# The first expert stage of a four-layer network: rows gathered by a slot table, results scattered tile by tile, no zeroed scratch

## The chip, the cores and the metric

The kernel runs on one core of a Trainium2 chip. The metric is the device time of one execution in microseconds, and below it is the median of several. The profile is one execution; its engines are PE (TensorE: matmuls, with PEld for its weight loads), DVE (VectorE), ACT (ScalarE), POOL (GpSimd) and SP (SyncE, which here only issues transfers). A row that ends in q (SPq, POOLq) is a queue from which transfers are issued.

## What is computed

A stream x of 16 x 64 tokens (1024 tokens, 256 values each) goes through four layers. Each layer adds a cross attention over 16 contexts of 1601 rows, a second attention or a scan, and a feed-forward part. The change concerns the feed-forward part of layer 0, and one side job in the cross attention of layer 0:

```python
def _L0_ffn_ref(hidden_states, gate_w, gate_bias, Wg, Wu, Wd, Sg, Su, Sd):
    E = 64
    TOP_K = 8
...
    x = hidden_states.reshape(B * S, H)
    rw = _route(x, gate_w, gate_bias)
    expert_out = jax.vmap(lambda gw_, uw_, dw_: _mlp(x, gw_, uw_, dw_))(Wg, Wu, Wd)
    routed = jnp.einsum('eth,te->th', expert_out, rw)
    shared = _mlp(x, Sg, Su, Sd)
    out = (routed + shared).reshape(B, S, H)
```

Each token picks 8 of 64 experts, each expert is a small gated network (256 to 176 to 256), and one shared network of 352 hidden values runs for all tokens.

## The kernel before

The stages run one after the other, with a barrier between two of them. `routed_experts` (from L1392) is the stage of the experts. Its inputs are `xn` (`nf_xn` in the profile), the 1024 normalised tokens as 8 tiles of 128 rows, the routing weights `score` and the choice `mask`. The 8192 pairs of a token and one of its experts are sorted by expert; each expert's pairs fill whole tiles of 128 slots, which needs at most `ROUTED_TILES` = 127 tiles, and all 127 are always computed. `owner_i` holds the expert of each tile, and `slot_i` (`e_sloti`) the slot of each pair.

In order:

- DVE computes slots and owners in a chain of short operations (`link` waits for each), fed by two matmuls that count the mask (L1561, L1562). These wait for the two constants on `const_in`.
- PE, ACT and DVE run a software pipeline over `UNITS` = 16 + 127 units: 16 shared units (two per token tile, weights `ws`), then one unit per routed tile. In loop step n, PE turns the rows of unit n+3 (`turn`, L1519), multiplies gate and up of unit n+2 (`gate_up`, L1532), turns the hidden values of n+1 (`turn_hidden`, L1541) and multiplies down of unit n (`down`, L1555). DVE copies turned rows (`take_rows`), multiplies gate by up (`multiply`), and takes results (`take_output`).
- The rows reach their slots through DRAM: POOL scatters `xn` to `routed_x` with 64 indirect transfers of 128 rows of 1 KB (L1500), then SP loads `routed_x` in 16 loads of 8 tiles (`load_rows`, L1465). Results go in 32 stores of 4 tiles to `routed_y` (L1491).
- SP's loop waits for `y_ready` of tile j, then loads the weights of tile j+7 (L1469, 608 KB), and at times rows or results.
- When everything is stored, POOL gathers back with 64 indirect transfers (L1507), and DVE adds each of them, scaled by the pair's weight, to `x` (L1671). A ring of 16 buffers lies between.
- `find_weights` (L1649 to L1652, three DVE operations for each of 8 token tiles) finds the weight of each pair. It stands before the first `take_rows`.

Slots that no pair fills would hold what was in memory, so `routed_x` is set to zero before: in the cross attention of layer 0, SP writes 16 blocks of 1 MB of zeros (`x_zero`, L468) among the loads of the contexts, and POOL waits for `net.cleared` before its first scatter.

## Time and profile before

| | |
|---|---|
| time, median of 3 | 4475.74 us (4473.22 to 4480.47) |
| the profiled execution | 4455.4 us, its span 4453.6 us |
| PE busy | 3800.3 us, 85% of the span |
| DVE, ACT, POOL busy | 2224.7, 1781.0, 684.8 us |
| the stage of the experts | 928.5 to 1447.7 us of the span |
| mean granted TensorE clock | 0.919 of full speed |

The span counts from the first to the last recorded instruction; the time of the execution is 1.8 us longer. A row of the order of time begins with start and duration in us, then engine, line, operation, output and inputs; in brackets is how long its engine was idle before and what ended that. "issue" is idle time in which the engine waited for nothing that the profile shows. A row of a table of stretches has for each engine the busy us and the number of instructions, then the granted clock of PE (1.00 is full speed), the mean busy share of the 16 DMA engines, and GB/s.

### The profile page before, as it was taken

Reading aid. Unit: us, or ns where it says so; the run is one execution under the profiler, and the core shown is the slowest. Engines: PE = TensorE matmul, PEld = TensorE weight load, DVE = VectorE, ACT = ScalarE, POOL = GpSimd, SP = SyncE. Lnnn points to the kernel's source line nnn. Section 1 sums busy time; section 2 is a strip of 40 time slices with the busy share of each in tenths; the row PEclk is TensorE's granted clock in tenths of the full one; section 3 lists DMA queues with packets and bytes.
Section 4 is the critical chain, followed back from the end, with each engine's and each line's share of the span. In section 5 each row is a group of like instructions: output and inputs, shape, how many; then the busy total and the mean of one; then the engine's idle time right before and its main releaser. Section 6 shows DMA issues by size and latency. Waiting matters only on the chain. (4 is left out here: it accounts for less than half of the span.)

```text
span 4453.6 us, 141607 instructions
## 1 busy us (share of the span) xinstructions
PE 3800.3 (85%) x64078; PEld 2972.4 (67%) x64078; DVE 2224.7 (50%) x4259; ACT 1781.0 (40%) x3676; POOL 684.8 (15%) x393
## 2 busy tenths in 40 slices
PE   7999998647992799999966889999963789999988
PEld 5777776525771588888725568777843678878865
DVE  4555554542443555555564355555544255555543
ACT  4555453211220345454413345555531244544431
POOL 1111110031005111111140011111112111111100
PEclk9999999668996899999987899999976899999998
DMA  3121210026994211111040111111013611010001
GB/s 102 51 84 58 68 60 12 8 102 241 352 351 133 62 47 35 47 37 45 3 114 2 32 60 47 40 40 47 18 27 140 207 53 48 33 48 33 34 11 33
DMA packets 109045, 330.29 MB, mean 74 GB/s; under 512 B 31680, under 2 KB 55760, under 8 KB 101632
## 3 DMA queue, kind: packets, MB, share of 16 engines
q1 hardware_dynamic: 98800, 299.61, 20.0%
q0 software_dynamic: 6912, 18.88, 1.3%
q8 instruction: 507, 8.31, 0.8%
q10 hardware_dynamic: 2736, 2.75, 0.2%
q14 instruction: 90, 0.74, 0.1%
HBM read 261.80 MB, written 51.00 MB: 70 GB/s over the span
## 5 line engine op out<-in xcount | busy, mean ns | idle before, releaser
L636 DVE TENSOR_REDUCE x_pm<-banks 128x4 f32<-128x1536 f32 (+2 forms) x512 | 935.6, 1827 | 1034.7 <-PE banks L547 1034.7
L759 ACT ACTIVATE x_kT<-banks,x_bk 128x384 f32<-128x384 f32 (+2 forms) x512 | 305.1, 596 | 915.1 <-PE banks L589 915.1
L744 ACT ACTIVATE x_pe<-banks 128x512 f32<-128x512 f32 (+1 forms) x1024 | 474.2, 549 | 194.2 <-PE banks L527 194.2
L576 PE MATMUL banks<-x_wh,x_ch 128*128 128x256 f32 (+1 forms) x1664 | 523.6, 315 | 9.7 <-issue 5.8
L482 POOL TENSOR_TENSOR x_cl<-xnT,x_ch 128x1601 fp32r<-128x1601 f32 x60 | 218.6, 3643 | 1769.5 <-ACT x_ch L749 1769.5
L744 ACT ACTIVATE x_pl<-banks 128x384 f32<-128x384 f32 x1024 | 419.8, 496 | 166.9 <-PE banks L527 166.9
L576 PE MATMUL banks<-x_wh,x_cl 128*128 128x256 f32 (+1 forms) x1664 | 470.3, 283 | 1.7 <-issue 1.6
L527 PE MATMUL banks<-x_q,x_kT 32*128 32x128 f32 x13312 | 470.9, 274 | 0.5 <-issue 0.5
L576 PE MATMUL banks<-x_wl,x_ch 128*128 128x256 f32 (+1 forms) x1664 | 468.5, 282 | 1.7 <-issue 1.5
L576 PEld LDWEIGHTS banks<-x_wh,x_ch 128*128 128x128 f32 (+1 forms) x1664 | 307.9, 185 | 206.1 <-ACT x_pl L744 94.4
L547 PE MATMUL banks<-x_kT,x_q 32*128 32x384 f32 (+2 forms) x4096 | 434.7, 497 | 11.3 <-ACT x_kT L759 4.5
L527 PEld LDWEIGHTS banks<-x_q,x_kT 32*128 32x128 f32 x13312 | 427.0, 182 | 3.1 <-issue 0.8
L589 PE MATMUL banks<-x_ch,x_wh 128*128 128x384 f32 (+2 forms) x1024 | 370.9, 362 | 45.0 <-DVE x_cl L730 43.9
L669 DVE TENSOR_TENSOR x_v<-banks,x_bv 128x256 f32<-128x256 f32 (+1 forms) x832 | 320.4, 417 | 171.5 <-PE banks L576 171.2
L589 PE MATMUL banks<-x_ch,x_wl 128*128 128x384 f32 (+2 forms) x1024 | 358.8, 350 | 0.0
L589 PE MATMUL banks<-x_cl,x_wh 128*128 128x384 f32 (+2 forms) x1024 | 358.2, 350 | 0.0
L576 PEld LDWEIGHTS banks<-x_wl,x_ch 128*128 128x128 f32 (+1 forms) x1664 | 309.3, 186 | 2.8 <-issue 2.8
L576 PEld LDWEIGHTS banks<-x_wh,x_cl 128*128 128x128 f32 (+1 forms) x1664 | 309.2, 186 | 1.7 <-issue 1.7
L561 PEld LDWEIGHTS banks<-x_pl,x_v 128*32 128x32 f32 (+1 forms) x12288 | 182.4, 110 | 114.4 <-ACT x_pe L744 78.0
L561 PEld LDWEIGHTS banks<-x_pe,x_v 128*32 128x32 f32 x14336 | 206.8, 110 | 75.9 <-ACT x_pl L744 69.4
L561 PE MATMUL banks<-x_pe,x_v 128*32 128x64 f32 x14336 | 228.8, 220 | 15.0 <-issue 5.0
L561 PE MATMUL banks<-x_pl,x_v 128*32 128x64 f32 (+1 forms) x12288 | 206.1, 221 | 40.4 <-issue 24.9
(371 smaller groups left out, 5538.6 us busy)
## 6 DMA issues: line engine op xcount, KB each, us to landing
e_w<-in_L_pack SPq DMA_DIRECT2D x127, 608.0 KB, 6.6
xnT<-in_ctxT SPq DMA_DIRECT2D x64, 800.5 KB, 4.4
x_raw<-in_ctxT SPq DMA_DIRECT2D x60, 800.5 KB, 5.8
e_w<-in_L_pack SPq DMA_DIRECT2D x21, 1154.0 KB, 7.5
routed_x<-x_zero SPq DMA_DIRECT2D x16, 1024.0 KB, 8.3
e_xt<-routed_x SPq DMA_DIRECT2D x16, 1024.0 KB, 8.0
routed_y<-e_y SPq DMA_DIRECT2D x32, 512.0 KB, 7.5
a_swap<-a_raw SPq DMA_DIRECT2D x64, 128.0 KB, 2.3
```

Of the source, the lines that this page charges most:

```text
L482: nc.gpsimd.tensor_tensor(cl[:, b % 2, k, 0:CTX], staged(b, k), ch[:, b % 2, k, 0:CTX], ALU.subtract).then_inc(low_done, 1)
L527: last = nc.tensor.matmul(mine[j][0:n, (t - lo) * P:(t - lo + 1) * P], kT[r, c, t * P:t * P + n], qb[r, u, c], start=False, stop=True, ski ...
L547: last = nc.tensor.matmul(into[j][:, 0:hi - lo], qb[r, u, c], kT[r, c, lo:hi], start=not masked, stop=True, skip_group_check=masked)
L561: last = nc.tensor.matmul(bank[32 * j:32 * j + 32, e * S:(e + 1) * S], v[0:w, u, t, at:at + 32], probabilities(j, t, t + 1)[0:w, 0, e * S: ...
L576: last = nc.tensor.matmul(bank[0:w, (t - lo) * D:(t - lo + 1) * D], x[:, u, c, t * P:t * P + w], y[:, 1, c, :], start=(c == m == 0), stop= ...
L589: last = nc.tensor.matmul(bank[:, 0:hi - lo], w[:, 0, i, c * P:(c + 1) * P], x[:, u, i, lo:hi], start=(i == n == 0), stop=(i == KC - 1 and ...
L636: nc.vector.tensor_reduce(pm[:, c, :, g], net.quads[1 - k % 2][:, :, 0:hi - lo], AX.X, ALU.max).then_inc(max_done, 1)
L669: ins = nc.vector.tensor_tensor(heads, bank[0:w, (t - lo) * D:(t - lo + 1) * D].rearrange("p (h e f) -> p h e f", e=2, f=16), bvb[0:w].rea ...
L744: nc.scalar.activation(probabilities(j, lo, hi).rearrange("p t q -> p (t q)"), sets[k % 2][j][:, 0:(hi - lo) * P], ACT.Exp).then_inc(exp_d ...
L759: nc.scalar.activation(kT[:, c, lo:hi], sets[k % 2][key_bank(k)][:, 0:hi - lo], ACT.Identity, bias=col[:, c:c + 1]).then_inc(k_taken, 1)
```

## The change

- The zeros, their 16 writes and their semaphore are gone, and so is the scatter of `xn` by POOL. `xn` is written to `routed_x` as it is, 1 MB in one transfer by SP.
- A table is built that tells for each slot which pair fills it. For each token tile DVE makes 8 matrices `of_tile` (the pair's number where the column is the pair's tile) and 8 matrices `of_row` (1 where the column is the pair's row in its tile), 128 x 128 each, and PE adds the 64 products up in one PSUM tile (`index(t)`, in the first 8 shared units). DVE turns it into `to_pair` and `to_token`; an empty slot gets a spare row of its own behind the pairs. A third constant (`pair_rows`, 160 KB) is needed, and the first counting matmuls wait for it too.
- POOL gathers the rows of each tile by `to_token` into a ring of 8 and scatters the results of each tile by `to_pair` out of a ring of 8: 127 and 127 indirect transfers of 128 rows of 1 KB, in turn, inside the loop.
- Results lie in the order of token and pair afterwards, so that SP loads them back with 8 plain transfers of 1 MB into a ring of 4, and DVE's 64 additions alternate between two token tiles, each waiting for the addition two before it.
- SP's weight loads wait for `down_done` and no longer for `y_ready`. `find_weights` runs inside the loop, after the output of every eighth unit from the first routed one.

PE, place: the first shared units. `e_ws`, `xnT` are the shared weights and the turned tokens, `e_h` and `e_hT` the hidden values. Before:

```order
L1561 MATMUL banks<-r_mask,e_before 128x512
L1562 MATMUL banks<-r_mask,ones 128x512
L1564 MATMUL banks<-ident,e_owner 1x128
L1532 MATMUL banks<-e_ws,xnT 128x352 x4
L1541 MATMUL banks<-ident,e_h 88x128 x2
L1532 MATMUL banks<-e_ws,xnT 128x352 x2
L1541 MATMUL banks<-ident,e_h 88x128 x2
L1555 MATMUL banks<-e_ws,e_hT 128x256 x2
```

PE, the same place in the changed kernel:

```order
L1520 MATMUL banks<-e_ws,xnT 128x352 x4
L1551 MATMUL banks<-e_oftile,e_ofrow 128x128 x8
L1529 MATMUL banks<-ident,e_h 88x128 x2
L1520 MATMUL banks<-e_ws,xnT 128x352 x2
L1551 MATMUL banks<-e_oftile,e_ofrow 128x128 x8
L1529 MATMUL banks<-ident,e_h 88x128 x2
L1543 MATMUL banks<-e_ws,e_hT 128x256 x2
```

Eight matmuls of the table stand between gate-and-up and the turning of the hidden values, in each of 8 units. DVE, the same place in the changed kernel (`e_place` is the pair's tile and row, `e_h` the product of gate and up):

```order
L1613 CAST e_place<-e_sloti 128x128
L1615 TENSOR_SCALAR e_owneri<-banks 1x128
L1623 TENSOR_SCALAR e_oftile<-e_pair,e_place 128x128 x8
L1626 TENSOR_TENSOR e_ofrow<-e_pair,e_place 128x1024
L1647 TENSOR_TENSOR e_h<-e_g,banks 128x176
L1623 TENSOR_SCALAR e_oftile<-e_pair,e_place 128x128 x8
L1626 TENSOR_TENSOR e_ofrow<-e_pair,e_place 128x1024
L1647 TENSOR_TENSOR e_h<-e_g,banks 128x176
```

The two products of `multiply` have the making of the ones ahead of them now. POOL, the stage, before:

```order
L1495 UNCONDITIONAL_BRANCH
L1500 DMA routed_x<-nf_xn,e_sloti 16384x256 x64
L1507 DMA e_yt<-routed_y,e_sloti 128x256 x64
L40 UNCONDITIONAL_BRANCH
L43 ISA x2
```

POOL, the start of the stage in the changed kernel:

```order
L1490 MEMSET e_xt 128x2048
L1482 DMA e_xt<-routed_x,e_totoken 128x256 x9
L1487 DMA routed_y<-e_y,e_topair 24576x256
L1482 DMA e_xt<-routed_x,e_totoken 128x256
L1487 DMA routed_y<-e_y,e_topair 24576x256
```

Two blocks outside the loop became one gather and one scatter per tile inside it. The diff, cut to its core:

```diff
-                if clear is not None:
-                    for n in range(b * CLEARS // (B - 2), (b + 1) * CLEARS // (B - 2)):
-                        rows = clear[n * CLEAR_TILES * P:(n + 1) * CLEAR_TILES * P, :].rearrange("(p j) n -> p (j n)", p=P)
-                        sp.dma_start(rows, zero[:]).then_inc(net.cleared, 16)
...
-    LOAD, X_RING = 8, 3
-    STORE, Y_RING = 4, 2
-    RING = 16
+    X_RING, Y_RING, BACK = 8, 8, 4
+    PAIRED = TILES * K
...
             def load_weights(j):
                 e = sp.value_load(owner_i[0:1, j:j + 1], min_val=0, max_val=E - 1)
                 sp.dma_start(w[:, j % SLOTS], d["L0_pack"][bass.ds(e, 1)].rearrange("o p n -> p (o n)")).then_inc(w_in[j % SLOTS], 16)
 
             sp.dma_start(before[:], d["before"]).then_inc(const_in, 16)
             sp.dma_start(const[:], d["sort_rows"]).then_inc(const_in, 16)
+            sp.dma_start(pair[:], d["pair_rows"]).then_inc(const_in, 16)
             sp.dma_start(ws[:], d["L0_shared"].rearrange("s p n -> p s n")).then_inc(shared_in, 16)
+            sp.dma_start(x_rows.rearrange("(t p) n -> p t n", p=P), xn[:]).then_inc(rows_out, 16)
             sp.wait_ge(tiles_known, 1)
             for j in range(SLOTS):
                 load_weights(j)
-            sp.wait_ge(scattered, 16 * TILES * K)
-            for n in range(X_RING):
-                load_rows(n)
-            for j in range(ROUTED_TILES):
-                sp.wait_ge(y_ready, j + 1)
-                if j + SLOTS < ROUTED_TILES:
-                    load_weights(j + SLOTS)
-                if j % LOAD == 0 and j and j // LOAD + X_RING - 1 < LOADS:
-                    load_rows(j // LOAD + X_RING - 1)
-                n = j // STORE
-                tiles = tiles_of(n, STORE)
-                if j == tiles.stop - 1:
-                    at = tiles.start % LOAD
-                    rows = grouped(y_rows)[j // LOAD][:, at:at + STORE]
-                    sp.dma_start(rows, y[:, n % Y_RING]).then_inc(stored[n % Y_RING], 16)
+            for j in range(SLOTS, ROUTED_TILES):
+                sp.wait_ge(down_done, SHARED + j - SLOTS + 1)
+                load_weights(j)
             for s in range(Y_RING):
-                sp.wait_ge(stored[s], 16 * ((STORES - s + 1) // Y_RING))
+                sp.wait_ge(stored[s], 16 * uses(Y_RING, s))
+            for t in range(TILES):
+                if t >= BACK:
+                    sp.wait_ge(added, K * (t - BACK + 2 - t % 2))
+                rows = y_rows[t * P * K:(t + 1) * P * K, :].rearrange("(p k) n -> p (k n)", p=P)
+                sp.dma_start(yt[:, t % BACK].rearrange("p k n -> p (k n)"), rows).then_inc(back[t % BACK], 16)
 
         @block.gpsimd
         def _(pool):
-            pool.wait_ge(net.cleared, 16 * CLEARS)
-            pool.wait_ge(slots_known, 1)
-            for n in range(TILES * K):
-                pool.indirect_dma_start(x_rows, bass.IndirectOffsetOnAxis(ap=slot_i[:, n:n + 1], axis=0), xn[:, n // K, :],
-                                        None).then_inc(scattered, 16)
-            for s in range(Y_RING):
-                pool.wait_ge(stored[s], 16 * ((STORES - s + 1) // Y_RING))
-            for n in range(TILES * K):
-                if n >= RING:
-                    pool.wait_ge(added, n - RING + 1)
-                pool.indirect_dma_start(yt[:, n % RING, :], None, y_rows,
-                                        bass.IndirectOffsetOnAxis(ap=slot_i[:, n:n + 1], axis=0)).then_inc(back[n % RING], 16)
+            def gather(j):
+                s = j % X_RING
+                if j >= X_RING:
+                    pool.wait_ge(turned, j - X_RING + 1)
+                pool.indirect_dma_start(xt[:, s], None, x_rows, bass.IndirectOffsetOnAxis(ap=to_token[:, j:j + 1], axis=0)).then_inc(x_in[s], 16)
+
+            def scatter(j):
+                s = j % Y_RING
+                pool.wait_ge(y_ready, j + 1)
+                pool.indirect_dma_start(y_rows, bass.IndirectOffsetOnAxis(ap=to_pair[:, j:j + 1], axis=0), y[:, s],
+                                        None).then_inc(stored[s], 16)
+
+            nc.gpsimd.memset(xt[:], 0.0).then_inc(rows_out, 1)
+            pool.wait_ge(rows_out, 17)
+            pool.wait_ge(index_known, 1)
+            for j in range(X_RING):
+                gather(j)
+            for j in range(ROUTED_TILES):
+                if j + X_RING < ROUTED_TILES:
+                    gather(j + X_RING)
+                scatter(j)
...
+            def index(t):
+
+                pe.wait_ge(ones_made, 2 * t + 2)
+                for k in range(K):
+                    last = nc.tensor.matmul(table, of_row[:, t % 2, k], of_tile[:, t % 2, k], start=(t == k == 0),
+                                            stop=(t == TILES - 1 and k == K - 1))
+                last.then_inc(ones_used, 1)
...
-            pe.wait_ge(const_in, 32)
+            pe.wait_ge(const_in, 48)
...
-                if n + 3 == SHARED:
-                    pe.wait_ge(slots_known, 1)
-                    pe.wait_ge(tiles_known, 1)
                 if SHARED <= n + 3 < UNITS:
                     turn(n + 3)
                 if 0 <= n + 2 < UNITS:
                     gate_up(n + 2)
+                if 0 <= n + 1 < TILES:
+                    index(n + 1)
...
-            link(nc.vector.tensor_scalar(spot_i[:, 0], slot[:].rearrange("p t k -> p (t k)"), -1.0, None, ALU.add))
-            link(nc.vector.tensor_scalar(spot_i[:, 1], spot_i[:, 0], P - 1, 3, ALU.bitwise_and, ALU.logical_shift_left))
-            link(nc.vector.tensor_scalar(spot_i[:, 2], spot_i[:, 0], 7, LOAD - 1, ALU.logical_shift_right, ALU.bitwise_and))
-            link(nc.vector.tensor_scalar(spot_i[:, 3], spot_i[:, 0], LOADS * LOAD * P - LOAD * P, None, ALU.bitwise_and))
-            link(nc.vector.tensor_tensor(spot_i[:, 1], spot_i[:, 1], spot_i[:, 2], ALU.bitwise_or))
-            nc.vector.tensor_tensor(slot_i[:], spot_i[:, 1], spot_i[:, 3], ALU.bitwise_or).then_inc(slots_known, 1)
+            link(nc.vector.tensor_scalar(slot_i[:, 0], slot[:].rearrange("p t k -> p (t k)"), -1.0, None, ALU.add))
+            nc.vector.tensor_scalar(slot_i[:, 1], slot_i[:, 0], 7, None, ALU.logical_shift_right).then_inc(chain, 1)
+            link_two = nc.vector.tensor_scalar(slot_i[:, 2], slot_i[:, 0], P - 1, None, ALU.bitwise_and)
+            done[0] += 1
+            link(link_two)
+            link(nc.vector.tensor_copy(place[:], slot_i[:, 1:3]))
             dve.wait_ge(owner_turned, 1)
             nc.vector.tensor_scalar(owner_i[:], count[0:1, 0:P], -1.0, None, ALU.add).then_inc(tiles_known, 1)
+
+            def ones(t):
+
+                if t >= 2:
+                    dve.wait_ge(ones_used, t - 1)
+                for k in range(K):
+                    n = t * K + k
+                    ins = nc.vector.tensor_scalar(of_tile[:, t % 2, k], pair[:, PAIRED:PAIRED + P], place[:, 0, n:n + 1], pair[:, n:n + 1],
+                                                  ALU.is_equal, ALU.mult)
+                ins.then_inc(ones_made, 1)
+                nc.vector.tensor_tensor(of_row[:, t % 2], spread(pair[:, PAIRED:PAIRED + P].unsqueeze(1), (P, K, P)),
+                                        spread(place[:, 1, t * K:(t + 1) * K].unsqueeze(2), (P, K, P)), ALU.is_equal).then_inc(ones_made, 1)
+
+            def index():
+
+                dve.wait_ge(ones_used, TILES)
+                link(nc.vector.scalar_tensor_tensor(spare[:], table, 0.0, pair[:, PAIRED + P:], ALU.is_equal, ALU.mult))
+                link(nc.vector.scalar_tensor_tensor(to_pair[:], table, -1.0, spare[:], ALU.add, ALU.add))
+                nc.vector.tensor_scalar(to_token[:], to_pair[:], 3, TOK - 1, ALU.logical_shift_right, ALU.bitwise_and).then_inc(index_known, 1)
...
-                s = j // STORE
-                if s >= Y_RING:
-                    dve.wait_ge(stored[s % Y_RING], 16 * (s // Y_RING))
-                nc.vector.tensor_copy(y[:, s % Y_RING, j % STORE], y_ps[o % 2][:, 0:D]).then_inc(y_ready, 1)
+                if j >= Y_RING:
+                    dve.wait_ge(stored[j % Y_RING], 16 * (j // Y_RING))
+                nc.vector.tensor_copy(y[:, j % Y_RING], y_ps[o % 2][:, 0:D]).then_inc(y_ready, 1)
 
             def find_weights(t):
                 u = t % 2
...
 
             for n in range(-3, UNITS):
                 if SHARED <= n + 3 < UNITS:
-                    if n + 3 == SHARED:
-                        for t in range(TILES):
-                            find_weights(t)
                     take_rows(n + 3)
+                if 0 <= n + 2 < TILES:
+                    ones(n + 2)
+                if n + 2 == TILES:
+                    index()
                 if 0 <= n + 2 < UNITS:
                     multiply(n + 2)
                 if n >= 0 and (n >= SHARED or n % 2):
                     take_output(n)
+                if n >= SHARED and n % 8 == 0 and (n - SHARED) // 8 < TILES:
+                    find_weights((n - SHARED) // 8)
             dve.wait_ge(weighted, TILES)
             dve.wait_ge(shared_added, TILES)
             for n in range(TILES * K):
-                t, k = n // K, n % K
-                dve.wait_ge(back[n % RING], 16 * (n // RING + 1))
-                if k:
-                    dve.wait_ge(added, n)
-                nc.vector.scalar_tensor_tensor(net.x[:, t, :], yt[:, n % RING, :], weight[:, t, k:k + 1], net.x[:, t, :], ALU.mult,
+                t, k = 2 * (n // (2 * K)) + n % 2, n // 2 % K
+                if k == 0:
+                    dve.wait_ge(back[t % BACK], 16 * (t // BACK + 1))
+                else:
+                    dve.wait_ge(added, n - 1)
+                nc.vector.scalar_tensor_tensor(net.x[:, t, :], yt[:, t % BACK, k], weight[:, t, k:k + 1], net.x[:, t, :], ALU.mult,
                                                ALU.add).then_inc(added, 1)
```

## Rows read from the trace of the kernel before

**Rows 1.** Table of stretches, in the stage of the experts.

```profile
941.00:976.00 35.00, 33.91 (x142) 23.84 (x140) 12.21 (x41) 8.80 (x29) 22.66 (x24) 0.96 0.57 208
976.00:992.00 16.00, 0.00 (x0) 0.00 (x0) 15.31 (x24) 0.00 (x0) 12.62 (x12) 0.55 0.28 97
992.00:1030.00 38.00, 0.00 (x0) 0.00 (x0) 0.00 (x0) 0.00 (x0) 27.89 (x29) 0.50 0.30 104
1100.00:1150.00 50.00, 49.81 (x241) 36.73 (x240) 21.88 (x60) 11.97 (x40) 0.00 (x0) 1.00 0.98 351
1368.00:1447.00 79.00, 0.00 (x0) 0.00 (x0) 30.52 (x63) 0.00 (x0) 58.63 (x62) 0.50 0.36 105
```

**Rows 2.** Order of time: PE at the start and end of the routed units.

```profile
974.82 1.03 PE L1555 MATMUL banks<-e_ws,e_hT 88*128 88x256 f32 x4
...
1035.06 0.66 PE L1519 MATMUL banks<-ident,e_xt 128*128 128x128 f32 x2 [59.21 <-DMA e_xt<-routed_x]
...
1039.61 0.38 PE L1519 MATMUL banks<-ident,e_xt 128*128 128x128 f32 x2
...
1354.38 0.38 PE L1519 MATMUL banks<-ident,e_xt 128*128 128x128 f32 x2
```

**Rows 3.** Order of time: the end of the stage, last result to last addition.

```profile
1361.29 0.42 DVE L1645 COPY e_y<-banks 128x256 f32<-128x256 f32 x1 [0.44 <-PE banks L1555]
1365.20 0.98 POOL L1507 DMA_INDIRECT e_yt<-routed_y,e_sloti  x1 [336.49 <-DMA routed_y<-e_y]
...
1368.12 0.48 DVE L1671 SCALAR_TENSOR_TENSOR x_tok<-e_yt,e_weight,x_tok 128x256 f32<-128x256 f32 x1 [6.40 <-DMA e_yt<-routed_y,e_sloti]
...
1447.20 0.48 DVE L1671 SCALAR_TENSOR_TENSOR x_tok<-e_yt,e_weight,x_tok 128x256 f32<-128x256 f32 x1 [0.87 <-DMA e_yt<-routed_y,e_sloti]
```

**Rows 4.** POOL's indirect transfers: durations in ns, first and last start; two single ones.

```profile
L1500 POOL DMA_INDIRECT routed_x<-nf_xn,e_sloti x64: 959/963/1218, 946.3 to 1027.7; - x64
L1507 POOL DMA_INDIRECT e_yt<-routed_y,e_sloti x64: 949/949/985, 1365.2 to 1444.3; - x64
...
975.71 1.22 POOL L1500 DMA_INDIRECT routed_x<-nf_xn,e_sloti  x1 [0.30 <-issue]
```

**Rows 5.** Layer 0's cross attention: a write of zeros, a gap of PE, clock.

```profile
316.48 0.91 SPq L468 DMA_DIRECT2D routed_x<-x_zero  x2
325.79 0.43 PE L561 MATMUL banks<-x_pl,x_v 65*32 65x64 f32 x5 [2.83 <-issue]
322.90:325.80 2.90, 0.07 (x5) 0.01 (x3) 0.28 (x1) 0.00 (x0) 0.00 (x0) 1.00 0.96 398
325.80:329.50 3.70, 3.70 (x16) 3.14 (x17) 1.63 (x6) 0.00 (x0) 0.00 (x0) 0.54 0.05 18
```

**Rows 6.** The batches' results (L694) in the cross attention of layers 0 and 2.

```profile
L694 DVE TENSOR_TENSOR actT<-x_num,x_rec x16: 291/292/293, 119.2 to 740.1; 128x128 f32<-128x128 f32 x16
L694 DVE TENSOR_TENSOR actT<-x_num,x_rec x16: 291/292/293, 2659.5 to 3261.6; 128x128 f32<-128x128 f32 x16
```

**Rows 7.** Order of time: single operations whose kind or size the change uses.

```profile
908.85 4.44 DVE L1366 MAX8 r_top<-r_choice 128x8 f32<-128x8 f32 x64
921.27 1.11 DVE L1377 MAX8 r_best<-r_choice 128x8 f32<-128x64 f32 x8
...
928.88 0.43 SPq L1472 DMA_DIRECT2D e_const<-in_sort_rows  x1
930.64 2.07 PE L1561 MATMUL banks<-r_mask,e_before 128*128 128x512 f32 x2 [23.26 <-DMA e_const<-in_sort_rows]
...
945.93 0.42 PE L1541 MATMUL banks<-ident,e_h 128*88 128x128 f32 x2 [0.94 <-DVE e_h L1633]
...
1030.18 1.28 SPq L1465 DMA_DIRECT2D e_xt<-routed_x  x3
...
3445.80 1.95 PE L1800 MATMUL banks<-e_xT,e_w 128*128 128x128 f32 x16
```

**Rows 8.** Their landing, from issue in us, scatter; then the issues by kind.

```profile
DMA to landing us min/median/max: 2.4/2.6/11.0
e_yt<-routed_y,e_sloti POOLq DMA_INDIRECT x64, 2.8
e_w<-in_L_pack SPq DMA_DIRECT2D x127, 608.0 KB, 6.6
```

**Rows 9.** DMA queues: software queue in 992 to 1029 and 1368 to 1447.

```profile
q0 software_dynamic: 1392, 3.80, 29.6%
...
q0 software_dynamic: 3024, 8.26, 36.3%
```

More of the change, by code:

```diff
@@ L473, in _ @@
                 nc.gpsimd.memset(side[:].bitcast(F32), 1.0).then_inc(side_set, 1)
-            if clear is not None:
-                nc.gpsimd.memset(zero[:], 0.0).then_inc(zero_set, 1)
             for u in range(2):
@@ L1445, in routed_experts @@
         cum, count = net.bank(0), net.bank(1)
-        def tiles_of(n, size):
-            return range(n * size, min(n * size + size, ROUTED_TILES))
-        def grouped(rows):
-            return rows.rearrange("(g p j) n -> g p j n", p=P, j=LOAD)
+        table = net.bank(0)[:, 0:P]
         def weights(n):
@@ L2602, in arrange @@
                                a["L0_ffn_Sd"].reshape(D, 2, 176).transpose(1, 0, 2))
+    pairs = 8 * np.arange(TOK).reshape(TILES, P, 1) + np.arange(1, 9)
+    o["pair_rows"] = np.concatenate([pairs.transpose(1, 0, 2).reshape(P, -1), np.tile(np.arange(P), (P, 1)),
+                                      8 * TOK + 1 + p[:, None] + P * np.arange(P)], 1).astype(f)
     o["sort_rows"] = np.concatenate([np.tile(P * np.arange(8), (P, 1)), p[:, None]], 1).astype(f)
```

62 lines of the change are left out of this document (29 added, 33 removed).

## The prediction

> **What bounds the kernel now.** I read the table of stretches first. In the stage of the experts PE works through the shared units (941 to 976), stands still from 976 to 1030 at a granted clock of 0.50 to 0.55, is busy 49.8 of 50 us in the routed loop, and stands still again from 1368 to 1447 [rows 1]. The order of time gives the edges. The last shared product ends at 974.82 + 1.03 = 975.85; the first turning of routed rows starts at 1035.06, after 59.2 us on the rows' load [rows 2]. The last turning starts at 1354.38, the second at 1039.61, so a unit takes 314.8 / 125 = 2.52 us. The last result is copied at 1361.29 + 0.42 = 1361.7, and the last addition ends at 1447.2 + 0.5 = 1447.7: a tail of 86.0 us without PE [rows 3]. In both pauses POOL sets the pace: the scatter starts its 64 transfers between 946.3 and 1027.7, and the reads back theirs between 1365.2 and 1444.3, so 79.1 / 63 = 1.255 us each; a scatter issue lasts 0.963 and has the same 0.30 idle before it, 1.267 [rows 4]. So 145 us of this stage are POOL's pace with PE idle, and only the loop is PE's.
>
> The other part is the cross attention of layer 0, which writes zeros. PE stops there for 2.83 us on nothing that the profile shows, in a stretch in which the DMA engines move 398 GB/s, 6.5 us after two blocks of zeros were issued; in the next 3.7 us its clock is 0.54 [rows 5]. From first to last batch result this stage takes 740.1 - 119.2 = 620.9 us, and the same code without zeros in layer 2 takes 3261.6 - 2659.5 = 602.1 [rows 6]. I read the difference, 18.8 us, as the zeros' price.
>
> **The front of the stage.** The wait of 59.2 us goes: no scatter of 64 steps stands before the loop. Its place is taken by the table.
>
> A third constant delays the first counting matmul. Before, that matmul started 930.64 - 928.88 = 1.76 us after the issue of the second constant [rows 7]; one more issue is 0.48 us and 160 KB take about 0.4 at 398 GB/s, so I take 1.0 (bounds 0.5 and 2.5).
>
> DVE makes the ones. 64 operations on 8 values take 4.44 us, 0.069 each, and 8 on 64 values 1.11, with the last one's tail 0.13 each [rows 7]; so about 0.06 + 1.04 ns per value, and `ones` is 8 x 0.19 + 1.13 = 2.7 us (3.7 if its eight do not overlap). PE's share has a direct row: eight 128 x 128 products in two passes each take 1.95 us at full clock [rows 7]. DVE needs 2.7 + 0.34 + 0.42 = 3.5 us per unit, PE 2.30 + 1.95 = 4.25 (2.30 is (975.85 - 945.93) / 13), so PE sets the pace of the eight units, and DVE shows only once, before the first: `ones(0)` starts at about 946.3 and ends at 949.1, `index(0)` ends at 951.05, and the first turning of hidden values, at 945.93 before [rows 7], stands at 951.05. That is 5.1; the seven other index steps add 7 x 1.95 = 13.7. The first routed turning comes at 975.85 + 18.8 = 994.6 and not 1035.06: **40.4 us gained**. The bounds are 33 (DVE the pace, the first index at half clock, the constant late) and 44.
>
> Are the rows there by then? `index(7)` ends at 951.05 + 7 x 4.25 = 980.8, three short DVE operations make 981.8, and a gather lands 2.8 us after issue [rows 8]: 984.6, ten before PE asks. The eighth is issued at 990.6 and wanted at 994.6 + 7 x 2.52. The write of `xn` (1 MB, issued about 930) is long over.
>
> PE comes to the loop warm. Before, the first routed turning and the second lay 4.55 us apart [rows 2], against 2.52: **2.0 gained**.
>
> **The loop.** Per unit POOL now issues a gather and a scatter, 1.255 + 1.267 = 2.52 us, exactly PE's 2.52. A ring covers differences. POOL issues the gather of tile j+9 after the scatter of j, which is about 1.7 units after loop step j begins, and PE turns that tile at step j+6: 4.3 units or 10.7 us later, of which 2.8 to 4 go to landing. So 7 us of lag are covered. Against PE's undisturbed 2.49 POOL would fall behind by 0.03 x 119 = 3.8, and `find_weights` slows it: in 976 to 992, with DVE on such operations, an issue is up to 1.22 and not 0.96 [rows 4], two per call, 8 calls, at most 4. I put the remaining stall at **1 us lost**. `find_weights` itself was hidden in the 59 us; 24 operations of 0.64 us (15.31 / 24) [rows 1], 1.9 per call, now delay the copy of turned rows. DVE works 21.9 of 50 us in the loop [rows 1], and the copy has one unit of lead less its own 0.4, so some 0.3 of each 1.9 reaches PE: **2.4 lost** (bounds 0 and 15).
>
> The DMA engines: they are busy 0.97 to 0.98 of the loop at 351 GB/s. Of a unit's 864 KB, 256 change from bulk to rows of 1 KB. The software queue took 29.6% of 37 us for 29 scatters, 0.38 each, and 36.3% of 79 for 62 reads, 0.46 each [rows 9]; the same 256 KB in bulk are 0.98 x 2.49 x 256 / 864 = 0.72. The sum rises by 0.12 us per unit if the share is a true load, to 2.56, which would be 5 to 10 us lost. But 398 GB/s were moved in [rows 5], so the 0.98 is partly queueing; I take 0, and 10 as the bound.
>
> **The tail.** The last result is scattered (issued at once, landed in 2.6 to 2.8), and SP issues the first 1 MB at +2.9. Before, the first of three such loads was wanted 1035.06 - 1030.18 = 4.9 after its issue [rows 2, 7]; each further MB takes 2.6 at 398 GB/s. DVE's addition of 256 values is 0.33 us apart if two tiles alternate (0.06 + 0.27), 0.49 at its full duration. Tiles 0 and 1 are there at +7.8 and +10.4, their 16 additions end at +15.3, tiles 2 and 3 at +20.7. Tiles 4 and 5 are issued at +15.4, there at 20.3 and 22.9, added by +27.7; 6 and 7 are there by 28.3 and added by +33. I take 34, with 42 at 0.49 each. Against 86.0: **52 gained** (43 to 54).
>
> **The zeros.** If the gaps are theirs, 18.8 is gained; the context loads remain, so I take **17** (bounds 0 and 20). Nothing hangs on the change of SP's weight wait: it comes earlier by one DVE copy.
>
> **Sum.** 40.4 + 2.0 - 1 - 2.4 + 52 + 17 = 108 us. The profiled execution becomes 4455.4 - 108 = 4347; it was 20.3 under the median of the runs, so against the median the forecast is 4475.7 - 108 = 4368 us.
>
> Two rules of the Trainium skill speak about POOL's transfers. The page "DMA: Bandwidth & Descriptors", section "Anatomy of one DMA — SWDGE (gpsimd) path", fits 2.0 us plus bytes / 436e3 to one such transfer, 2.3 for 128 KB; in series two would make 4.6 per unit and about 260 us lost by estimate. The trace agrees with the figure as landing time (2.6 to 2.8) and not as pace (1.255), so the sum keeps the pace.
>
> **Rivals.**
> - *DVE holds POOL off in the loop; slower.* In 976 to 992 POOL's issue grew from 0.96 to 1.22 while DVE worked on SBUF [rows 4]. If each of the three DVE operations of a unit (0.42, 0.41, 0.34) held back a full descriptor writing, POOL would need 2.52 + 1.17 = 3.7 per unit: (3.7 - 2.52) x 127 - 7 = 143 lost, 4511 us. It decides from 2.52 + (108 + 7) / 127 = 3.4 per unit. Against it: 24 issues ran beside such operations from PSUM in the shared units, 22.66 us busy or 0.94 each [rows 1]. The skill's page "SBUF — State Buffer", section "SBUF: two separate sides", has this rule: GpSimd can't write descriptors while DVE runs a two-port operation, fp32 copy within SBUF above all. The loop's copies read PSUM, and the row of 1.22 agrees with it only for operations within SBUF. Chance 0.03.
> - *POOL is the bound by a little.* Two kinds of transfer in turn, each with a wait, cost 2.6 to 2.8: (0.08 to 0.28) x 127 - 7 = 3 to 29 lost, 4371 to 4397, more if late rows let PE's clock fall. For it: the sum is level with PE without any margin. Chance 0.17.
> - *The zeros cost nothing;* the gaps come from the code's place and the context loads, and reappear: 17 less, 4385. Against it: layer 2's 602.1. Chance 0.12.
> - *DMA-bound loop,* 10 lost, 4378. Chance 0.08.
> - *The table is late or the rows of gaps in later stages shift:* other parts unchanged in code take 10 more. Chance 0.03.
>
> **How the numbers follow.** The forecast has 0.57, with 4350 to 4385 as its own range. Low end: 44 + 2 + 54 + 20 gained is 120, and later stages' gaps may give a few: 4350. High end: front 33, loop 15 lost, tail 43, zeros 10 is 73, 4403. The range 4350 to 4405 leaves out 0.2. Only the first rival ends slower: faster by over 0.2% (9 us, about what runs of this kernel can tell) 0.96, within it 0.01, slower 0.03.
>
> **What would show it.** The wait of the first routed turning under 5 us and its start near 995; eight units of 4.25 before it; the second turning 2.5 after the first; turnings 2.5 apart and POOL's issues 1.26 apart, with no wait for `e_xt` above 1 us in the loop; 34 us from the last `e_y` to the last `x_tok` of the stage; layer 0's batches over 602 to 605 us with no gap above 2 us. Wrong it would be if POOL's pairs take over 2.6 us, if PE waits for `e_xt` or `e_w` in most units, or if the 2.8 us gaps remain.

## The result, and the profile after

The changed kernel takes **4408.05 us** (median of 4 runs, 4403.77 to 4413.44) against 4477.57 for the kernel before on the same chip: ratio 0.9844, 95% interval 0.9828 to 0.9860. That is 69.5 us faster, where I forecast 108 (4368, range 4350 to 4405). The profiled execution took 4404.97 us, span 4403.1; that of before took 4455.4. Between the two profiled executions the difference is 50.4, and it is this one that the stretches below must add up to.

The front of the stage, in order of time (columns as in [rows 2]):

```profile
908.92 0.43 SPq L1458 DMA_DIRECT2D e_const<-in_sort_rows  x1
911.70 1.22 PE L1557 MATMUL banks<-r_mask,e_before 128*128 128x512 f32 x1 [24.28 <-DMA e_pair<-in_pair_rows]
926.14 2.12 DVE L1623 TENSOR_SCALAR e_oftile<-e_pair,e_place 128x128 f32<-128x128 f32 x8
928.18 1.21 DVE L1626 TENSOR_TENSOR e_ofrow<-e_pair,e_place 128x1024 f32<-128x1024 f32 x1
950.61 1.95 PE L1551 MATMUL banks<-e_oftile,e_ofrow 128*128 128x128 f32 x16
962.44 1.12 POOL L1482 DMA_INDIRECT e_xt<-routed_x,e_totoken  x1 [52.09 <-DVE e_totoken L1634]
975.32 0.39 PE L1508 MATMUL banks<-ident,e_xt 128*128 128x128 f32 x2
977.81 0.39 PE L1508 MATMUL banks<-ident,e_xt 128*128 128x128 f32 x2
```

The issue of the second constant stands at 908.92, against 928.88 [rows 7]: the stage starts 20.0 us earlier, and that is layer 0, whose batches' results (line 694 before, 684 now) last 720.4 - 119.2 = 601.2 us against 620.9 [rows 6]. From that issue to the first routed turning it is 66.4 us now and was 106.2 [rows 2, 7]: 39.8 gained, with no wait on the rows. The second turning comes 2.49 later.

```profile
L684 DVE TENSOR_TENSOR actT<-x_num,x_rec x16: 291/292/293, 119.2 to 720.4; 128x128 f32<-128x128 f32 x16
```

The tail (DVE waits four times for a load there, 11.7 us in all; two of the four are shown):

```profile
1366.31 0.42 DVE L1658 COPY e_y<-banks 128x256 f32<-128x256 f32 x1 [0.44 <-PE banks L1543]
1367.59 0.96 POOL L1487 DMA_INDIRECT routed_y<-e_y,e_topair  x1 [0.30 <-issue]
1370.14 2.14 SPq L1474 DMA_DIRECT2D e_yt<-routed_y  x4
1375.07 0.48 DVE L1688 SCALAR_TENSOR_TENSOR x_tok<-e_yt,e_weight,x_tok 128x256 f32<-128x256 f32 x1 [8.34 <-DMA e_yt<-routed_y]
1398.05 6.03 DVE L1688 SCALAR_TENSOR_TENSOR x_tok<-e_yt,e_weight,x_tok 128x256 f32<-128x256 f32 x15 [0.83 <-DMA e_yt<-routed_y]
```

From the end of the last copy, 1366.73, to 1398.05 + 6.03 = 1404.1 it is 37.4 us, against 86.0 [rows 3]: 48.6 gained. But between the first turning at 975.3 and the last at 1359.4 lie 384.1 us, against 1354.4 - 1035.1 = 319.3 [rows 2]: **64.8 lost**. Sum: 19.7 + 39.8 - 64.8 + 48.6 = 43.3, and the stages behind it give the other 7. Table of stretches (PE, PEld, DVE, ACT and POOL busy, PEclk, DMA share, GB/s), in the loop:

```profile
1100.00:1150.00 50.00, 43.87 (x199) 31.44 (x199) 21.33 (x56) 10.39 (x34) 31.68 (x32) 0.97 0.83 284
1200.00:1250.00 50.00, 44.04 (x191) 29.79 (x189) 17.33 (x47) 9.29 (x30) 32.08 (x33) 0.97 0.84 289
```

PE is busy 44 of 50 us and not 49.8, and nothing else has become full [rows 1]: the DMA engines fell from 0.98 to 0.83, POOL is at 32 of 50. The second row lies behind `find_weights`, and stalls just as the first does. No bound shows in this table, so one stall must be read in order of time:

```profile
1187.10 0.34 DVE L1647 TENSOR_TENSOR e_h<-e_g,banks 128x176 f32<-128x176 f32 x1 [1.00 <-issue]
...
1187.86 1.35 PE L1520 MATMUL banks<-e_w,e_xT 128*128 128x352 f32 x4
...
1189.05 0.97 POOL L1482 DMA_INDIRECT e_xt<-routed_x,e_totoken  x1 [0.31 <-issue]
1189.26 1.03 PE L1543 MATMUL banks<-e_w,e_hT 88*128 88x256 f32 x4
...
1190.32 0.98 POOL L1487 DMA_INDIRECT routed_y<-e_y,e_topair  x1 [0.30 <-issue]
1190.36 1.42 PE L1520 MATMUL banks<-e_w,e_xT 128*128 128x352 f32 x4
1191.61 0.97 POOL L1482 DMA_INDIRECT e_xt<-routed_x,e_totoken  x1 [0.30 <-issue]
1192.68 0.32 ACT L1698 ACTIVATE e_g<-banks 128x176 f32<-128x176 f32 x1 [5.33 <-PE banks L1520]
...
1193.43 0.42 PE L1529 MATMUL banks<-ident,e_h 128*88 128x128 f32 x2 [1.64 <-issue]
...
1194.16 0.43 DVE L1658 COPY e_y<-banks 128x256 f32<-128x256 f32 x1 [0.80 <-remote]
...
1194.87 0.98 POOL L1487 DMA_INDIRECT routed_y<-e_y,e_topair  x1 [2.29 <-DVE e_y L1658]
```

The gate and up product that starts at 1187.86 ends at 1189.21, but ACT, whose other wait (for `e_h`) was over at 1187.44, takes it at 1192.68. The down product ends at 1190.29, and DVE copies it at 1194.16. Then POOL, which had issued without a pause, gets its result, 2.29 us late. So what is late is TensorE's *signal*. I counted it from the trace's semaphore events, between 1050 and 1290 us: how long after the end of a product its increment is recorded. Before: 380 of 380 increments, mean 0.01 us, longest 0.02. After: 265 recorded for 309 products, 148 of them later than 0.1, mean 0.99, longest 4.73. Each increment is held against the latest product before it, so these delays are lower bounds. The increments of DVE and ACT that are recorded stand 0.01 us after their instructions, but over a third of those (DVE 93 of 249, ACT 54 of 156) are missing from the trace, so of them it is not shown.

POOL's issues have a pattern too: often six or eight, 1.28 us apart, then about 3 us to the next.

### The profile page after: what moved, and what is told of

Read it like the earlier page. It is cut to its first block and busy times, and to the rows that moved or that the text cites. A ratio compares the mean times of both kernels' runs of the same rounds, so it can differ in the third digit from the quotient of the medians.

```text
span 4403.1 us, 141949 instructions
## 1 busy us (share of the span) xinstructions
PE 3827.4 (87%) x64206; PEld 2983.3 (68%) x64206; DVE 2240.8 (51%) x4332; ACT 1781.4 (40%) x3676; POOL 809.2 (18%) x519
## 5 line engine op out<-in xcount | busy, mean ns | idle before, releaser
L472 POOL TENSOR_TENSOR x_cl<-x_raw,x_ch 128x1601 fp32r<-128x1601 f32 x60 | 181.0, 3017 | 368.5 <-ACT x_ch L739 368.5
```

Source lines behind the costliest of these rows:

```text
L472: nc.gpsimd.tensor_tensor(cl[:, b % 2, k, 0:CTX], staged(b, k), ch[:, b % 2, k, 0:CTX], ALU.subtract).then_inc(low_done, 1)
```

## The experiments

Each expectation is quoted as it stood before its run; the letters of the theories are explained where they first come. In the end theory D, which limits the number of indirect transfers in this loop to about one per 1.5 us, is what the runs left standing; it names no mechanism. Times are medians of 4 runs; "loop" is the time from the first to the last routed unit's down product, 126 units (314.0 us before, 380.8 in the changed kernel); "late" counts TensorE's increments between 1050 and 1290 us that were late as above, of those recorded.

**Plain loads.** SP loads 128 rows at a fixed place for every tile:

```diff
-                pool.indirect_dma_start(xt[:, s], None, x_rows, bass.IndirectOffsetOnAxis(ap=to_token[:, j:j + 1], axis=0)).then_inc(x_in[s], 16)
+                sp.dma_start(xt[:, s], x_rows[t * P:(t + 1) * P, :]).then_inc(x_in[s], 16)
```

> The changed kernel with its 128 row gathers made plain loads of 128 rows on SP's queue (the same 128 KB each, wrong rows, so the output is not the reference's); the 128 scatters stay on POOL. Measured in the changed kernel: 3.05 us per routed unit against 2.49 to 2.52 before, and 92 to 103 recorded signals of each kind of TensorE's (semaphore increments) that arrive with a median delay of 0.24 to 0.87 us and up to 4.7 us after the end of the matmul, against 0.02 us in the kernel before. Theory A (two indirect issues per unit, 1.28 us apart, hold TensorE's signals back, which then pass one every 0.74 us or so, four per unit): with one indirect issue per unit POOL pauses 1.2 us in each unit and the signals catch up: 2.5 to 2.6 us per unit, whole time 4345 to 4360. Theory B (the DMA engines have too much to do with weights, rows and results together): the bytes are the same, 4395 to 4410. Theory C (POOL's own pace of 2.56 us per unit, and its catching up): half the issues, 4340 to 4350, with no late signals at all.

4344.5 us, ratio to before 0.9710 (0.9694 to 0.9727). Loop 314.2, late 0 of 369.

**Plain stores.**

```diff
-                pool.indirect_dma_start(y_rows, bass.IndirectOffsetOnAxis(ap=to_pair[:, j:j + 1], axis=0), y[:, s],
-                                        None).then_inc(stored[s], 16)
+                sp.dma_start(y_rows[j * P:(j + 1) * P, :], y[:, s]).then_inc(stored[s], 16)
```

> The changed kernel with its 128 scatters made plain stores of 128 rows in slot order on SP's queue (results then stand at wrong rows, so the output is not the reference's); the 128 gathers stay on POOL. Theory A: as with plain loads, one indirect issue per unit, 2.5 to 2.6 us per unit, 4345 to 4360; if only one of the two kinds of indirect transfer delays TensorE's signals, this run and the one with plain loads differ by most of 60 us. Theory B: 4395 to 4410. Theory C: 4340 to 4350 and no late signals.

4344.0 us, 0.9711 (0.9695 to 0.9727). Loop 314.2, late 0 of 272. The table for this kernel in the same stretch:

```profile
1100.00:1150.00 50.00, 49.54 (x239) 36.49 (x238) 25.06 (x66) 11.95 (x40) 19.13 (x20) 1.00 1.01 348
```

**Both plain.** Both edits at once.

> The changed kernel with both gathers and scatters made plain transfers of the same size on SP's queue (output not the reference's), so that no indirect transfer is left in the routed stage. All theories but B: the loop runs at the 2.49 us per unit of before, with signals 0.02 us late, 4335 to 4345. Theory B (bytes on the DMA engines): still near 3 us per unit, 4395 to 4410. It also gives the floor for the loop with these waits, buffers and rings.

4346.4 us, 0.9708 (0.9687 to 0.9729). Loop 314.2. So the same bytes through the same engines cost nothing, and theory B falls; one indirect transfer per unit, of either kind, costs nothing either. The 64.8 us come back when either is gone. Theory C, POOL's own pace, stands so far.

**Two signals.** One increment for a turning and the down product ahead of it (`edge`), and one for the gate and up product and the turning of hidden values (`middle`):

```diff
-                last.then_inc(turned, 1)
+                last.then_inc(edge, 1)
...
-                last.then_inc(down_done, 1)
+                if not SHARED <= n + 4 < UNITS:
+                    last.then_inc(edge, 1)
...
-                last.then_inc(gu_full, 1)
+                if n == 0:
+                    last.then_inc(middle, 1)
...
-                last.then_inc(h_turned, 1)
+                last.then_inc(middle, 1)
```

> The changed kernel with nothing left out, but TensorE signals twice per unit in place of four times: the signal of a turn stands for the down product ahead of it too, and that of a hidden turn for the gate and up product ahead of it. Each consumer waits for the joint signal, 0.2 to 0.4 us later than needed. Theory A: two signals at 0.74 us are 1.5 us per unit, under TensorE's 2.49, so signals no longer set the pace; POOL's 2.56 us do: 126 x (3.05 - 2.56) = 62 us come back, 4340 to 4360. Theories B and C: the transfers and POOL's work are unchanged, and the joint signals come later: 4405 to 4425.

4408.5 us, 0.9850 (0.9827 to 0.9872): no change, loop 378.0, 67 late of 138. I had read a queue of signals that drains by 0.74 us each; halving them would have halved that. It didn't, so theory A in this form fell. POOL's rows show what is constant, eight issues and a pause of 2.23 us before the ninth, 12.17 us for eight issues or 1.52 each:

```profile
1247.73 0.98 POOL L1487 DMA_INDIRECT routed_y<-e_y,e_topair  x1 [2.23 <-DVE e_y L1660]
1249.02 0.97 POOL L1482 DMA_INDIRECT e_xt<-routed_x,e_totoken  x1 [0.30 <-issue]
...
1256.70 0.97 POOL L1482 DMA_INDIRECT e_xt<-routed_x,e_totoken  x1 [0.30 <-issue]
1259.90 0.98 POOL L1487 DMA_INDIRECT routed_y<-e_y,e_topair  x1 [2.23 <-DVE e_y L1660]
```

**Slower TensorE.**

```diff
-                for c in range(KC):
+                for c in [*range(KC)] * 2:
                     last = nc.tensor.transpose(x_ps[j % 2][:, c * P:(c + 1) * P], xt[:, j % X_RING, c * P:(c + 1) * P], net.ident[:])
```

> The changed kernel with both row turnings of a unit done twice (the same writes again), so that TensorE's own unit grows from 2.49 to about 2.49 + 2 x 0.11 = 2.71 us and stands above the 2.56 us of POOL's pair of issues. The runs before showed: one indirect issue per unit costs nothing (4344 with either kind plain, as with both plain), and half as many signals of TensorE's change nothing (4408.5). Theory P (the signals are held only when POOL has no pause between issues, which comes about because 2.56 is above 2.49; then all engines stand until POOL runs out of work): more work for TensorE makes the loop faster: 2.71 to 2.75 us per unit, 4408 - 126 x (3.05 - 2.73) = 4368, range 4360 to 4380. Theory D (each indirect transfer costs the software queue 1.52 us behind its 0.97 us issue, 3.05 us per pair): no change, 4400 to 4412. Theory W (software queue and weights share the DMA engines, and the 1 KB rows hold them up): no change or a little slower, 4400 to 4430.

4412.0 us, 0.9862 (0.9841 to 0.9882). Loop 388.2, 137 late of 273. A TensorE that is slower than POOL's pair of issues doesn't help, as theory D said and P denied. Theory C falls with P: if POOL's 2.56 us per pair were the limit, TensorE's 2.71 would now set the pace and the loop would last 341 us.

**Seven of eight.** SP loads every eighth tile of rows plainly; POOL leaves it out:

```diff
-                if j + X_RING < ROUTED_TILES:
+                if j + X_RING < ROUTED_TILES and j % 8 != 8 - 1:
                     gather(j + X_RING)
```

> The changed kernel with one gather in eight made a plain load of 128 rows on SP's queue (wrong rows for these tiles, so the output is not the reference's): POOL issues 1.875 indirect transfers per unit, 1.875 x 1.28 = 2.40 us, just under TensorE's 2.49. Theory P: POOL has a pause in nearly every unit, 2.5 us per unit, 4344 to 4356. Theory D: 1.875 x 1.52 = 2.85 us per unit, 4408 - 126 x 0.20 = 4383, range 4375 to 4392. Theory W: bytes and rows fall by little, 4395 to 4408.

4391.8 us, 0.9815 (0.9794 to 0.9835). Loop 366.3 with 239 transfers in place of 254, 138 late of 257. P wanted 4344 to 4356; D's 4383 is 9 too low, its sign and most of its size are right (239 x 1.52 = 363).

**Few weights.** SP's loop of weight loads is gone, and PE waits only for the first seven.

```diff
-            for j in range(SLOTS, ROUTED_TILES):
-                sp.wait_ge(down_done, SHARED + j - SLOTS + 1)
-                load_weights(j)
```

> The changed kernel with the weights of the first 7 routed units used for all (no weight load in the loop, output not the reference's): the hardware queue is silent there, 608 of the 864 KB of a unit are gone, and the 256 indirect transfers stay. Theory W: 2.56 us per unit, 4340 to 4355, no late signals of TensorE's. Theories P and D: 3.05 us per unit as before, 4400 to 4412, the signals up to 4 us late as before.

4403.1 us, 0.9841 (0.9821 to 0.9861). Loop 376.3, 148 late of 259. The 5 us below the changed kernel are within the noise (0.9841 against 0.9844). The DMA engines are now three quarters idle, and PE stalls as before:

```profile
1100.00:1150.00 50.00, 44.23 (x201) 30.74 (x200) 21.95 (x58) 11.07 (x36) 31.27 (x32) 1.00 0.26 82
```

Theory W falls: neither weights nor bytes are in it.

**Zeros back.** The 16 writes and their semaphore as in the kernel before, onto a scratch of their own:

```diff
+                if clear is not None:
+                    for n in range(b * CLEARS // (B - 2), (b + 1) * CLEARS // (B - 2)):
+                        rows = clear[n * CLEAR_TILES * P:(n + 1) * CLEAR_TILES * P, :].rearrange("(p j) n -> p (j n)", p=P)
+                        sp.dma_start(rows, zero[:]).then_inc(net.cleared, 16)
```

> The changed kernel with the 16 writes of zeros put back into the cross attention of layer 0, on a scratch of their own that nothing reads and nothing waits for. It isolates one term of the sum: I forecast 17 us for it, and the changed kernel's stage of the experts begins 20 us earlier. If the zeros are the price, 4408 + 17 to 20 = 4425 to 4428; if the code's place or the context loads make the 2.8 us gaps, 4408.

4428.2 us, 0.9904 (0.9878 to 0.9930): 20.1 more than the changed kernel, and the second constant is issued at 928.90, where it was before. The zeros' price is shown, 20 us. With them come back four of TensorE's gaps on nothing that the profile shows, 2.0 to 3.2 us long (ending at 197.0, 325.2, 454.7 and 583.0), in the places where the kernel before has four of 2.65 to 2.83 and the changed one none.

**Light TensorE.** One of the two steps of each routed product:

```diff
-                for k in range(KC):
+                parts = KC if j < 0 else 1
+                for k in range(parts):
```

> The changed kernel with half of TensorE's gate, up and down products of the routed units left out (output not the reference's), so that its unit is about 1.5 us and all transfers, waits and copies stay. So far: the routed loop of the changed kernel lasts about 380 us with TensorE's unit at 2.49 or at 2.71, with all weights or none, with two signals or four; with 239 indirect transfers in place of 254 it lasts 364, and with 127 it is TensorE's 312. Theory D (the software queue sustains one indirect transfer per 1.5 us when both kinds pass through it): still 3.0 us per unit, 4395 to 4410. Theory T (TensorE's work takes something from POOL's transfers, since the 64 scatters and 62 reads of the kernel before stood 1.27 and 1.255 us apart with TensorE idle): with half its work 2.6 to 2.8 us per unit, 4350 to 4380.

4400.2 us, 0.9817 (0.9800 to 0.9835). Loop 371.9, 142 late of 239, still 2.95 us per unit and not the 2.6 to 2.8 of theory T.

```profile
1100.00:1150.00 50.00, 34.93 (x129) 22.55 (x129) 22.06 (x56) 10.61 (x33) 31.44 (x33) 0.77 0.82 274
```

The test is weaker than planned. The granted clock fell from 0.97 to 0.77, so TensorE's busy time fell from 43.9 to 34.9 of 50 us and not by 40%. A weaker effect of TensorE's work isn't excluded. The expectation is also wrong on one point: 24 of the kernel before's 64 scatters did not stand with TensorE idle (see "What stays open").

**Two gathers, and two scatters.** Each transfer of the one kind is issued once more, between a buffer and a ring of its own; the other kind is plain:

```diff
+                pool.indirect_dma_start(xt2[:, s], None, x_rows, bass.IndirectOffsetOnAxis(ap=to_token[:, j:j + 1], axis=0)).then_inc(again[s], 16)
```

> The kernel with plain stores (4344 us) with every gather of the routed loop issued a second time, into a ring of its own that nobody reads (output not the reference's): again 254 indirect transfers, all of one kind. Theory D as a matter of number: 3.0 us per unit, 4400 to 4415. If the alternation of gather and scatter is what costs, a loop of gathers alone runs at 2 x 1.25 = 2.5 us per unit, 4344 to 4356.

4417.1 us, 0.9866 (0.9847 to 0.9886), loop 387.3.

> The kernel with plain loads (4344 us) with every scatter of the routed loop issued a second time, from a buffer of zeros into a scratch that nobody reads (output not the reference's): 254 indirect transfers, all scatters. By number alone: 3.0 us per unit, 4400 to 4415. If it is the gathers that are dear (eight gathers in a row at the start of the kernel with plain stores made TensorE's signals 1.8 us late, and the scatters of the kernel before made none late), 2.53 us per unit, 4344 to 4356. If alternation is what costs, 4344 to 4356 too, and then the run with two gathers tells the two apart.

4424.4 us, 0.9874 (0.9848 to 0.9900), loop 393.1. In this loop neither kind is cheap, and alternation is not the cause; the number is. The 9 and 16 us above the changed kernel are not explained.

**Read back by index.** Plain stores, and the 64 gathers of the kernel before at the end:

```diff
+            for n in range(TILES * K):
+                if n >= BACK:
+                    pool.wait_ge(added, n - BACK + 1)
+                pool.indirect_dma_start(yt[:, n % BACK, :], None, y_rows,
+                                        bass.IndirectOffsetOnAxis(ap=slot_i[:, 0, n:n + 1], axis=0)).then_inc(back[n % BACK], 16)
```

> A whole kernel with nothing left out: rows gathered tile by tile as in the changed kernel, results stored plainly in slot order on SP's queue, and read back at the end by 64 indirect gathers as in the kernel before. One indirect transfer per unit in the loop, so it keeps TensorE's 2.49 us (4344 with plain stores), and the tail grows from 35 back to 86 us. Theory D and T alike: 4344 + 51 = 4395, range 4388 to 4402, some 13 us less than the changed kernel.

**4392.2 us**, 0.9809 (0.9791 to 0.9826), the best whole kernel, 16 us less than the changed one. Loop 314.2, late 0 of 292; from the last result to the last addition 84.6 us. Its tail also shows that POOL alone can go at its short pace, with TensorE idle: 56 issues in 70 us, 1.25 each, as in [rows 1, 4].

```profile
1310.00:1380.00 70.00, 0.00 (x0) 0.00 (x0) 27.13 (x56) 0.00 (x0) 53.02 (x56) 0.50 0.36 105
```

**Half the rows.** Three more runs asked where the limit lies.

```diff
-                pool.indirect_dma_start(xt[:, s], None, x_rows, bass.IndirectOffsetOnAxis(ap=to_token[:, j:j + 1], axis=0)).then_inc(x_in[s], 16)
+                pool.indirect_dma_start(xt[0:P // 2, s], None, x_rows, bass.IndirectOffsetOnAxis(ap=to_token[0:P // 2, j:j + 1], axis=0)).then_inc(x_in[s], 16)
```

> The changed kernel with its gathers cut to the first 64 rows of each tile (the other rows stay zero, so the output is not the reference's); the number of issues stays 254, the rows fall by a quarter. If the limit goes by rows written by the software queue: (64 + 128) / 256 x 3.05 = 2.29 us per unit, under TensorE's 2.49, no stalls, 4344 to 4352. If it goes by transfers: 3.0 us per unit, 4400 to 4410.

4418.0 us, 0.9842 (0.9820 to 0.9864), loop 382.7, 163 late of 279. It goes by transfers, not by rows. The median is 8 above the range for transfers; that is not explained (the four runs spread from 4405 to 4418).

**Every other gather plain.** As seven of eight, with 2 in place of 8.

> The changed kernel with every other gather a plain load on SP's queue (wrong rows there, output not the reference's): 1.5 indirect transfers per unit. If 1.5 us per transfer is the limit as an average: 1.5 x 1.52 = 2.28 us per unit, under 2.49, no late signals, 4344 to 4352. If any two issues close together do harm, half of the units stall: 4370 to 4380.

4340.6 us, 0.9691 (0.9666 to 0.9716). Loop 314.2 with 191 transfers, late 29 of 231, the longest by 1.34 us, and the loop is no longer for it. Three issues in a row stand 1.27 us apart here, so three that close do no harm.

**TensorE at three.** Both turnings four times.

> The changed kernel with both row turnings done four times, so that TensorE's own unit is 2.49 + 6 x 0.11 = 3.15 us and POOL's two issues have 1.57 us each on average, though they may still stand 1.28 apart. Average limit: no stalls, 126 x 3.15 = 397 us of loop, 4408 + 13 = 4421, signals 0.02 us late. If any two issues close together do harm, the stalls of about 60 us come on top: 4460 to 4480.

4421.4 us, 0.9861 (0.9838 to 0.9880). Loop 400.7, and PE has no idle time in the stretch shown:

```profile
1100.00:1150.00 50.00, 50.00 (x288) 39.74 (x287) 22.39 (x54) 9.50 (x32) 31.26 (x33) 1.00 0.91 282
```

65 of 241 increments are late, up to 2.81 us, but the 3.15 us unit has room for them.

## Why the prediction was wrong

**The step that failed** is in the loop: "Per unit POOL now issues a gather and a scatter, 1.255 + 1.267 = 2.52 us, exactly PE's 2.52." Both numbers are spacings of issues in long bursts [rows 4], and they were used as the pace of a loop in which POOL and TensorE wait for each other. In the loop POOL still issues 1.28 us apart, but often after six to eight issues TensorE's signals stay out, the others stand still for want of them, and POOL too when its next result is missing. Over bursts and gaps a pair took 3.05 us and not 2.52. Kernels with 254 indirect transfers had loops of 372 to 393 us in nine cases (the changed one and eight of the experiments). 243 of the transfers are issued within the loop (250 with two scatters), so that is 1.53 to 1.60 us each. TensorE's own need ranged meanwhile from about 260 us (126 x 2.06, estimated from its busy share with the light TensorE, 34.9 of 50 us at 2.95 per unit) to 341 (126 x 2.71). With 239 transfers the loop took 366. 191 and 127 fitted into TensorE's 314, and with a TensorE unit of 3.15 us the transfers no longer set the pace. I forecast 3.4 us lost and 2.0 gained between the first and the last turning, and 64.8 were lost.

**The rival that came nearest** was "POOL is the bound by a little": its side was right, its 2.6 to 2.8 us per pair too small against 3.05, since it too was built on the short spacing and small additions. The rival that DVE holds POOL off is not what happened: issues last 0.97 us in the loop, as alone [rows 4]. Nor is the DMA-bound loop: the share fell, and taking the weights away changed 5 us.

**The Trainium skill's rule** that I weighed against the trace, in "DMA: Bandwidth & Descriptors", section "Anatomy of one DMA — SWDGE (gpsimd) path", gives a fit of 2.0 us plus bytes / 436e3 for one transfer; by estimate that is 2.3 us for 128 KB and 4.6 for two in series. The landings in the kernel before, 2.6 to 2.8 us [rows 8], are 0.3 to 0.5 above its figure for one transfer. As a pace per unit the 4.6 is half again too slow (3.05 measured), and my own 2.52 was too fast.

**Term by term.** *Front:* 40.4 forecast, 39.8 measured up to the first routed turning; `index` took the 1.95 us of [rows 7], and the ones 2.12 + 1.21 = 3.3 where I forecast 2.7. *Warm clock:* 2.0 forecast; the second turning came after 2.49 and not 4.55, 2.06, shown (it is inside the 64.8, which without it are 66.9). *`find_weights`:* 2.4 forecast; not separated, since the loop stalls with and without it; plain loads kept it and ran at 314.2 from first to last product, where the kernel before took 314.0, so its loss was small or none. *Tail:* 52 forecast, 48.6 measured; the first load came 8.34 us after DVE's last copy ended, and the additions took 6.03 / 15 = 0.40 each, where I had 0.33. *Zeros:* 17 forecast, 20 measured twice, in the trace and by putting them back. *Median:* I set the sum against a profiled execution that lay 20.3 us under the median of its runs and carried those 20 over; the changed kernel's profiled execution lies 3.1 under its median. That hid a part of the miss: with the loop as forecast the changed kernel would stand near 4346, as "both plain" does, and my 4368 would have been 22 too high.

**What stays open:** why TensorE's increments stay out. Shown is that in this loop it goes by the number of transfers, and not by kind, rows, bytes, weights or the number of increments. In the stall shown the delay is real and not one of the records alone: the late increments stand at 1192.66 and 1194.14, and ACT and DVE start 0.02 us after them. Whether DVE's and ACT's own increments are held too can't be read, as over a third of them are missing.

Two bursts outside the loop narrow it down, and neither theory D nor T accounts for them. In the changed kernel POOL issues eight gathers in a row, 1.25 us apart, while TensorE still works on the shared units and waits for none of them; between 971 and 974 four of TensorE's increments come 0.2 to 1.68 us late. Eleven experiments have seven or eight gathers in a row there, plain stores and read back by index among them, and each has three or four late increments, the longest by 1.94 us. With four in a row (every other gather plain) none is late. In the kernel before, 24 scatters start 1.27 us apart beside TensorE's shared units, with PE busy 33.9 of 35 us [rows 1], and all 41 of TensorE's increments recorded between 944 and 976 are on time. So close issues beside a working TensorE are not enough by themselves. Those 24 scatters all signal one semaphore, and POOL waits for nothing between them; the transfers of the changed kernel signal sixteen semaphores in turn, and in its loop the engines wait for each other. The loop with two scatters per unit was late all the same, so it is not the kind of transfer alone. No run changed the semaphores or the waits by themselves, and that is the rival left to test.

## What to carry to other kernels

Price an operation where it will stand: the spacing of issues in a burst is a lower bound of their cost in a loop, even where TensorE was busy beside the burst, as it was for 24 of the scatters. When a change moves indirect transfers into a loop with TensorE's work, count them against the time of the loop: here at one per 1.66 us (1.5 per unit) they were free, and a loop that wanted them faster than one per 1.5 us took 1.53 to 1.60 us for each. Of two sets of such transfers, leave the one outside that is fewer: with the 64 reads at the end the tail is 47 us longer (84.6 against 37.4), with 127 more scatters the loop is 67 us longer (380.8 against 314.2). When every engine has room and yet all stand still together, compare the end of the producing instruction with the start of its consumer.

## What the runs showed of the hardware

Between 1050 and 1290 us, every recorded semaphore increment of TensorE stood 0.01 to 0.02 us after the product's end in the kernels with up to one indirect transfer per 2.49 us, and up to 7.61 us after it with two gathers per unit. Outside that stretch, seven or eight gathers in a row ahead of the loop made three or four increments 0.2 to 1.94 us late, also where the loop had one transfer per unit; 24 scatters in a row in the kernel before made none late. The issue itself showed nothing: it mostly lasted 0.95 to 0.98 us with and without late signals. Halving the rows of the gathers shortened their issue only from 0.97 to 0.92 us. More work for TensorE, two to four times the turnings, made the kernel at most 13 us slower: most of it filled time in which the engine had waited.
